# Four of sixteen feed-forward inputs transposed through DRAM and VectorE instead of TensorE, on one Trainium2 core

## The reference

```python
x = x + 0.5 * ffn(layernorm(x))      # "first"
x = x + attention(layernorm(x))      # "att"
x = x + 0.5 * ffn(layernorm(x))      # "second"

def ffn(x):                          # W_fc 512 x 128, W_proj 128 x 512
    y = square(relu(x @ W_fc.T)) @ W_proj.T
    # five steps of a leaky spiking neuron driven by y; the share of steps that spike
    return spike_count(y) / 5        # a staircase of y with five levels

def attention(x):                    # a second layer norm with gamma, beta inside
    h = layer_norm(x) * gamma + beta
    keys, values = h @ Wk.T + bk, h @ Wv.T + bv
    w = exp((keys @ Wka.T + bka) / sqrt(128))
    w = w / cumsum(w, over tokens)
    return cumsum(w * keys, over tokens) * values
```

## Time and profile before

| | |
|---|---|
| median of 3 runs | 148.91 us (148.85 to 149.03) |
| profiled execution | 148.56 us, of which the span from first to last instruction is 146.8 us |
| TensorE busy | 141.6 us, 96% of the span |
| VectorE busy | 128.8 us, 88% |
| ScalarE busy | 128.5 us, 88% |
| GpSimd busy | 95.1 us, 65% |
| granted TensorE clock | 1.000 of full speed (2.4 GHz) over the whole span |

### The profile page before, as it was taken

How to read it: one execution, slowest core, us unless ns; L and a number is a source line. 1 busy time by engine, 2 the same in 40 slices (tenths; PEclk the granted TensorE clock), 3 DMA queues, 4 the chain that set the end, 5 groups by cost and what they waited for, 6 DMA issues and landing times.

```text
span 146.8 us, 3000 instructions
## 1 busy us (share of the span) xinstructions
PE 141.6 (96%) x945; PEld 126.1 (86%) x945; DVE 128.8 (88%) x441; ACT 128.5 (88%) x255; POOL 95.1 (65%) x138
## 2 busy tenths in 40 slices
PE   7899999999999999999999999999999999999990
PEld 7599898989889889997988988889989898979780
DVE  2985478999699999999989999999989999968674
ACT  3376989999999998979999999899898988988861
POOL 1448135478899928993999899998934954580200
PEclk9999999999999999999999999999999999999999
DMA  4975000000000000000000000000000101040422
GB/s 136 273 195 165 4 2 0 0 0 7 0 0 2 2 4 0 0 0 0 4 0 2 0 0 4 2 0 0 0 4 0 55 18 58 18 143 0 143 71 72
DMA packets 10510, 5.09 MB, mean 35 GB/s; under 512 B 1152, under 2 KB 10496, under 8 KB 10496
## 3 DMA queue, kind: packets, MB, share of 16 engines
q1 hardware_dynamic: 9808, 4.53, 10.7%
q10 hardware_dynamic: 688, 0.39, 0.9%
HBM read 2.82 MB, written 2.10 MB: 34 GB/s over the span
## 4 chain that ended last, share of the span: by engine, by line
PE 92%; DMA 3%; DVE 1%; ACT 1%; ACTq 1%; issue 0%
PE work L1062 37%; PE hidden L983 11%; PE hidden L987 10%; PE hidden L984 10%; PE work L996 5%; DMA proj_raw<-in_L_ffn_W_proj_dram 3%; PE att_work L1093 3%; PE att_work L983 3%; PE att_work L984 3%; PE att_work L987 3%; PE att_value L1117 2%; PE att_value L983 1%; PE att_value L987 1%; PE att_value L984 1%; PE work L1074 1%; ACT signs L535 1%
## 5 line engine op out<-in xcount | busy, mean ns | idle before, releaser
L1062 PE MATMUL work<-proj_t,square 128*128 128x128 f32 x480 | 61.7, 276 | 0.1
L1062 PEld LDWEIGHTS work<-proj_t,square 128*128 128x128 f32 x480 | 59.0, 192 | 2.9 <-POOL square L455 0.5
L551 ACT ACTIVATE signs<-work 128x512 uint8<-128x512 f32 x63 | 35.7, 619 | 5.3 <-PE work L1062 5.3
L522 ACT ACTIVATE relu<-hidden 128x512 f32<-128x512 f32 x64 | 38.0, 627 | 0.0
L527 ACT ACTIVATE square<-relu 128x512 f32<-128x512 f32 x53 | 35.5, 670 | 0.3
L983 PE MATMUL hidden<-in_hi,fc_lo 128*128 128x512 f32 (+1 forms) x66 | 27.6, 418 | 0.1
L429 POOL TENSOR_TENSOR rstd<-var_eps,minus_half 128x4 f32<-128x4 f32 x15 | 15.3, 1021 | 16.2 <-DVE neg_mean L646 16.2
L987 PE MATMUL hidden<-in_lo,fc_hi 128*128 128x512 f32 (+1 forms) x66 | 25.6, 388 | 0.0
L984 PE MATMUL hidden<-in_hi,fc_hi 128*128 128x512 f32 (+1 forms) x66 | 25.4, 385 | 0.0
L435 POOL TENSOR_SCALAR normed<-x_second,neg_mean,rstd 128x128 f32<-128x128 f32 x32 | 16.7, 534 | 0.8
L435 POOL TENSOR_SCALAR normed_att<-x_att,neg_mean_att,rstd_att 128x128 f32<-128x128 f32 x28 | 16.2, 590 | 0.7
(11 more groups left out here) (123 smaller groups left out, 257.8 us busy)
## 6 DMA issues: line engine op xcount, KB each, us to landing
x_first<-_attn_hidden_states_dram SPq DMA_DIRECT2D x7, 256.0 KB, 4.4
out_dram<-x_out SPq DMA_DIRECT2D x7, 256.0 KB, 2.2
out_dram<-x_out SPq DMA_DIRECT2D x4, 64.0 KB, 1.5
x_first<-_attn_hidden_states_dram ACTq DMA_DIRECT2D x1, 128.0 KB, 2.7
x_first<-_attn_hidden_states_dram SPq DMA_DIRECT2D x1, 128.0 KB, 2.4
fc_raw<-in_L_ffn_W_fc_dram SPq DMA_DIRECT2D x1, 128.0 KB, 2.7
fc_raw<-in_L_ffn_W_fc_dram ACTq DMA_DIRECT2D x1, 128.0 KB, 3.3
proj_raw<-in_L_ffn_W_proj_dram SPq DMA_DIRECT2D x1, 128.0 KB, 3.5
```

What stands on the lines that cost most here:

```text
L522: nc.scalar.activation(relu[j.lane][:, c, :], bank_of_hidden(j, c)[:], ACT.Relu).then_inc(relu_made[j.lane], 1)
L551: nc.scalar.activation(planes[:, k, :], work[j.lane][:], func, bias=bias, scale=scale).then_inc(signs_made[j.lane], 1)
L1062: last = nc.tensor.matmul(work[j.lane][:, tokens], square[j.lane][:, c, tokens], proj_t[:, c, :], start=(c == 0 and t == 0), stop=(c == NC ...
```

## The change

Jobs 4 to 7 no longer go through TensorE for their transpose. `normed` is stored to a DRAM scratch and loaded back by four DMAs so that each 32 x 32 block lies in the place of its transpose, and VectorE's block transpose turns all the blocks at once (`turn_by_dma`, `turn_blocks`). `ff_hi` then reads this SBUF tile; it stands earlier in ScalarE's step, right behind `ff_relu(i, 2)`. The low part moves from VectorE to GpSimd (`ff_pool_lo`). Each of these jobs has normalisation buffers of its own, and its layer norm is computed earlier: on VectorE, job 4 in step 1, job 5 in step 2, jobs 6 and 7 in step 3; on GpSimd, job 4 in iteration 0, job 5 in iteration 1, job 6 in iteration 2 and job 7 in iteration 3. To make room, `x_of["att"]` and `x_of["out"]` become the same buffers as `x_of["first"]` and `x_of["second"]`, so that the residual adds write in place.

```diff
+DMA_TURNED = (4, 5, 6, 7)
+BLOCK = 32
...
+        self.dma_turned = i in DMA_TURNED
+        self.norm = f"dma{i}" if self.dma_turned else self.lane
+        self.norm_turn = 0 if self.dma_turned else sum(k not in DMA_TURNED for k in range(self.lane, i, 2))
...
-        KINDS = (0, 1, "att")
+        KINDS = (0, 1, "att") + tuple(FeedForward(i).norm for i in DMA_TURNED)
...
-        x_of = {k: [sb(f"x_{k}_{b}", [P, NT, P]) for b in range(NB)] for k in ("first", "att", "second", "out")}
+        x_of = {k: [sb(f"x_{k}_{b}", [P, NT, P]) for b in range(NB)] for k in ("first", "second")}
+        x_of["att"], x_of["out"] = x_of["first"], x_of["second"]
...
+            def turn_by_dma(j):
+
+                i, rows, columns = j.index, S // BLOCK, D // BLOCK
+                sp.wait_ge(normed_made[j.norm], NT)
+                sp.dma_start(scratch[i].rearrange("(t p) d -> p t d", p=P),
+                             normed[j.norm][:]).then_inc(normed_stored[i], 16)
+                sp.wait_ge(normed_stored[i], 16)
+                source = scratch[i].rearrange("(i r) (j c) -> j r i c", r=BLOCK, c=BLOCK)
+                for k in range(columns):
+                    sp.dma_start(blocks[i][k * BLOCK:(k + 1) * BLOCK, :].rearrange("r (i c) -> r i c", i=rows),
+                                 source[k]).then_inc(blocks_loaded[i], 16)
+
+            for i in DMA_TURNED:
+                turn_by_dma(FeedForward(i))
...
+            def ff_pool_lo(j):
+                pool.wait_ge(blocks_turned[j.index], 1)
+                pool.wait_ge(hi_made[j.lane], j.turn + 1)
+                pool.wait_ge(hidden_made[j.lane], NC * j.turn)
+                nc.gpsimd.tensor_tensor(in_lo[j.lane][:], turned_x[j.index][:], in_hi[j.lane][:].bitcast(F32),
+                                        ALU.subtract).then_inc(lo_made[j.lane], 1)
...
             for i in range(FIRST_STEP, STEPS):
                 for j in feed_forward(i + 2):
-                    ff_normalise(j)
+                    if not j.dma_turned and j.index != 3:
+                        ff_normalise(j)
+                if i == 0:
+                    ff_normalise(FeedForward(4))
+                if i == 1:
+                    ff_normalise(FeedForward(3))
+                if i == 2:
+                    ff_normalise(FeedForward(6))
+                if i == 3:
+                    ff_normalise(FeedForward(7))
+                for j in feed_forward(i + 2):
+                    if j.dma_turned:
+                        ff_pool_lo(j)
                 for b in attention(i + 2):
                     att_normalise(b)
+                if i == 1:
+                    ff_normalise(FeedForward(5))
...
-                act.wait_ge(turned[j.lane], j.turn + 1)
+                if j.dma_turned:
+                    act.wait_ge(blocks_turned[j.index], 1)
+                    act.wait_ge(hidden_made[j.lane], NC * j.turn)
+                    nc.scalar.activation(in_hi[j.lane][:], turned_x[j.index][:], ACT.Copy).then_inc(hi_made[j.lane], 1)
+                    return
...
                     ff_square(j, 1)
                     ff_relu(j, 2)
+                for j in feed_forward(i + 1):
+                    if j.dma_turned:
+                        ff_hi(j)
...
+            def ff_layer_norm(j):
+                ff_layer_stats(j)
+                ff_layer_args(j)
+
+            def turn_blocks(j):
+                dve.wait_ge(blocks_loaded[j.index], 16 * (D // BLOCK))
+                nc.vector.transpose(turned_x[j.index][:], blocks[j.index][:]).then_inc(blocks_turned[j.index], 1)
...
                 if i == ATT_STEP[0]:
                     first_attention_normalise()
+                    ff_layer_stats(FeedForward(6))
...
+                if i == ATT_STEP[0]:
+                    ff_layer_args(FeedForward(6))
...
                 for j in feed_forward(i):
-                    if j.index > 0:
+                    if j.index > 0 and not j.dma_turned:
                         ff_lo(j)
+                if i == 1:
+                    ff_layer_norm(FeedForward(4))
+                if i == 2:
+                    ff_layer_norm(FeedForward(5))
...
                 for b in attention(i):
                     att_part_lo(b)
+                for j in feed_forward(i + 1):
+                    if j.dma_turned:
+                        turn_blocks(j)
...
                 for b in attention(i):
                     att_sum(b)
+                if i == 3:
+                    ff_layer_norm(FeedForward(7))
...
             def ff_turn(j):
 
+                if j.dma_turned:
+                    return
...
             def ff_contract(j, c):
+                if j.dma_turned and c == 0:
+                    pe.wait_ge(signs_made[j.lane], j.before(lambda other: other.sign_parts))
```

More of the change, by code:

```diff
@@ L206, in macaron_kernel @@
     FIRST_STEP = -3
-    EPS_OF = {0: LN_EPS, 1: LN_EPS, "att": LN_EPS * LN_EPS / (1.0 + LN_EPS)}
+    ATT_EPS = LN_EPS * LN_EPS / (1.0 + LN_EPS)
     ATT_GAMMA_SCALE = 1.0 / math.sqrt(1.0 + LN_EPS)
@@ L266, in macaron_kernel @@
         normed = {k: sb(f"normed_{k}", [P, NT, P]) for k in KINDS}
+        assert S % BLOCK == 0 and D % BLOCK == 0
+        blocks = {i: sb(f"blocks{i}", [P, S]) for i in DMA_TURNED}
+        turned_x = {i: sb(f"turned_x{i}", [P, S]) for i in DMA_TURNED}
+        scratch = {i: nc.dram_tensor(f"scratch{i}", (S, D), F32) for i in DMA_TURNED}
         in_hi = [sb(f"in_hi{l}", [P, S], F32R) for l in LANES]
@@ L333, in macaron_kernel @@
         pooled_made, attended_made, attended_turned = sem("pooled_made"), sem("attended_made"), sem("attended_turned")
+        normed_stored = {i: sem(f"normed_stored{i}") for i in DMA_TURNED}
+        blocks_loaded = {i: sem(f"blocks_loaded{i}") for i in DMA_TURNED}
+        blocks_turned = {i: sem(f"blocks_turned{i}") for i in DMA_TURNED}
         def flat(tile):
@@ L441, in ff_normalise @@
                 else:
-                    normalise(j.lane, j.turn, x_of[j.layer][j.batch])
+                    normalise(j.norm, j.norm_turn, x_of[j.layer][j.batch])
+            def ff_pool_lo(j):
[4 more added lines that the diff above has]
+                                        ALU.subtract).then_inc(lo_made[j.lane], 1)
             def att_normalise(b):
@@ L516, in ff_hi @@
                     return
-                act.wait_ge(turned[j.lane], j.turn + 1)
+                if j.dma_turned:
[3 more added lines that the diff above has]
+                    return
+                act.wait_ge(turned[j.lane], j.norm_turn + 1)
                 nc.scalar.activation(in_hi[j.lane][:], work[j.lane][:], ACT.Copy).then_inc(hi_made[j.lane], 1)
@@ L621, in _ @@
                 for j in feed_forward(i + 1):
-                    ff_hi(j)
+                    if not j.dma_turned:
+                        ff_hi(j)
                     if j.index == 0:
@@ L672, in ff_layer_stats @@
                     dve.wait_ge(x_made["second"], j.batch + 1)
-                layer_stats(j.lane, j.turn, x_of[j.layer][j.batch])
+                layer_stats(j.norm, j.norm_turn, x_of[j.layer][j.batch])
             def ff_layer_args(j):
-                layer_args(j.lane, j.turn)
+                layer_args(j.norm, j.norm_turn)
+            def ff_layer_norm(j):
[4 more added lines that the diff above has]
+                nc.vector.transpose(turned_x[j.index][:], blocks[j.index][:]).then_inc(blocks_turned[j.index], 1)
             def att_layer_stats(b):
@@ L897, in _ @@
             for kind in KINDS:
-                nc.vector.memset(moments[kind][:, :, 2:3], EPS_OF[kind]).then_inc(consts_made, 1)
+                nc.vector.memset(moments[kind][:, :, 2:3], ATT_EPS if kind == "att" else LN_EPS).then_inc(consts_made, 1)
             nc.vector.memset(ones[:, P:S], 1.0).then_inc(consts_made, 1)
@@ L917, in _ @@
                         other_fc_low_parts()
-                    else:
+                    elif not j.dma_turned:
                         ff_layer_stats(j)
@@ L993, in ff_turn @@
                 for t in range(NT):
-                    pe.wait_ge(normed_made[j.lane], NT * j.turn + t + 1)
+                    pe.wait_ge(normed_made[j.norm], NT * j.norm_turn + t + 1)
                     bank_of = first_second_half if j.index == 0 and t >= HALF_TILES else work[j.lane]
-                    last = nc.tensor.transpose(bank_of[:, t * P:(t + 1) * P], normed[j.lane][:, t, :], ident[:])
+                    last = nc.tensor.transpose(bank_of[:, t * P:(t + 1) * P], normed[j.norm][:, t, :], ident[:])
                     if j.index == 0 and t == HALF_TILES - 1:
@@ L999, in ff_turn @@
                         turn_proj(range(0, NC // 2))
-                last.then_inc(turned[j.lane], 1)
+                last.then_inc(turned[j.norm], 1)
             def turn_proj(chunks):
```

## The result

The changed kernel takes **155.67 us** (median of 6 runs, 155.40 to 157.04), the kernel before 148.95 us beside it (6 runs, 148.71 to 149.33). The ratio is 1.0464, with a 95% interval of 1.0431 to 1.0497: 4.6% slower. The forecast was 155.8 us.

A forecast was written before the change was run, and what follows sets the result against it. TensorE sets the pace, with ScalarE as full; the low part closes a loop of ScalarE and GpSimd. Delays reach 6.9 us: 148.56 + 6.9 = 155.5 us, by the median 155.8 us, range 150.5 to 158.4 us.

The forecast's parts named there:

- The closed loop: ScalarE and GpSimd wait for each other from step 4 on; one turn 11.6 us against 9.37 before; chance 0.73.
- the path of the sum: Delays of `att_turn` grow over steps 4, 5 and 7 to 6.9 us, which stays to the end.
- The lead of 0.6 us in step 2: VectorE does job 5's layer norm before `att_layer_stats(0)`, so `first_attention_normalise`, then TensorE and ScalarE, run 0.6 us late.
- the guess of step 6: On ScalarE, batch 2's guess comes 0.5 us later because `ff_hi(6)` now stands ahead of it.
- the listed sign: TensorE idle 2 us or more in front of L1093 in each of steps 4, 5 and 7, released by GpSimd.
- three signs of being wrong: TensorE idle under 1.8 us in steps 4 to 7; `in_hi` of job 4 well before 34 us; `turn_blocks` awaiting loads.
- The other signs: GpSimd idle ahead of the low part, `att_off_square` released by the guess sum, no VectorE DMA wait behind step 2.
- The block transposes at nothing: On VectorE, 0.7 us each, adding nothing because VectorE has 1.36 us to spare in step 4.
- The DMA path: Store lands in 2.2 us, the four loads in 3.5 to 8.8 us; taken as hidden.
- The late-loads rival: VectorE stops at `turn_blocks(5)` if the four loads take over 8.4 us; 159.4 us at 12 us; chance 0.05.
- The pure gain: `att_normalise` stays off the path and TensorE keeps its 1.76 us: 147.15 us; chance 0.11.
- Half of the loop: One or two of the three waits are covered as ScalarE runs ahead; step 4 alone gives 150.2 us; chance 0.09.

The follow-up runs named there:

- E1: The changed kernel with GpSimd's low part behind `att_normalise` instead of ahead of it, nothing else changed: 151.97 us.
- E9: The changed kernel with only job 6's low part on GpSimd, those of jobs 4, 5 and 7 back on VectorE: 151.92 us.
- E10: The changed kernel with only job 5's low part on GpSimd, those of jobs 4, 6 and 7 back on VectorE: 153.18 us.
- E2: The changed kernel with the low part of jobs 4 to 7 back on VectorE at its old place, reading SBUF: 152.03 us.
- E5: As E2, with `in_hi` of jobs 4 to 7 back near the end of ScalarE's step, behind the last square: 150.33 us.
- E4: The kernel before with only the earlier layer norms, their own buffers and in-place sums; transposes on TensorE, no DMA path: 149.68 us.
- E8: The kernel before plus four VectorE block transposes that nobody reads, one in each of steps 3 to 6: 151.74 us.
- E7: As E6, with `in_hi` of jobs 4 to 7 written by VectorE right behind the block transpose: 152.02 us.
- E6: As E5, with moved layer norms in slots of the kernel before, one step sooner, and block transposes behind `att_share_key`: 150.74 us.
- E3: The changed kernel with GpSimd doing each of the four low parts twice, the first into a tile nobody reads: 161.37 us.

## Why the prediction was right, step by step

*What sets the time.* The prediction said of the low part that "on GpSimd it stands in front of `att_normalise`, whose result those three `att_turn` wait for". This is shown by E1, where the order alone is worth 3.7 us, and by E9 against E10. But it is not the whole of the slowdown, as the prediction had it. The rest, about 3 us, came to light only in E1, E2 and E5.

*The closed loop.* One turn, from `att_off_square(0)` to `(1)`, took 54.31 - 42.98 = 11.33 us (predicted 11.6, before 9.37). `att_turn` was late by 2.62, 4.46 and 6.78 us (predicted 2.59, 4.52 and 6.89). `att_off_square(2)` came at 64.06 - 1.69 = 62.37 us (62.65), and in sum nothing was won or lost after step 7. So the path of the sum is the one that the trace shows. The durations held too: block transpose 0.70 us (0.7), low part 1.28 (1.27), `in_hi` 0.65 (0.63). `att_normalise` was 2.93, 2.90 and 3.04 us, near the lower bound, and not 3.29. That the sum is right to 0.1 us is in part luck: these three are 1.0 us shorter together than was added up, and most of that was paid back by a longer lead (0.77 us in place of 0.6) and by the way from the start of `in_hi` to the low part, 0.8 us in each turn in place of 0.63.

*The lead of 0.6 us in step 2.* Size about right, place wrong. `first_attention_normalise` starts at 29.19 - 1.69 = 27.50 instead of 27.33 us, only 0.17 later. The rest came in step 3: the low part of job 3 on VectorE stands behind the layer norm of job 6, and TensorE waits 0.43 us for it (L1069). ScalarE passed `ff_relu(3, 2)` at 36.76 - 1.69 = 35.07 instead of 34.30 us, 0.77 late. E4 prices the moved layer norms at 0.6 us in all.

*What the prediction didn't see.* It counted `in_hi` as a link of GpSimd's loop and, but for the guess of step 6, not as a cost for ScalarE's other customers. The signs, the square and the guess that now stand behind it come later, and TensorE waits for the square: 0.76 us in step 4, 0.46 in step 5, 0.24 and 0.46 in step 6, though no row of before shows such a wait. With the low part out of the way (E2) that is what gates, and moving `in_hi` back is worth 1.7 us (E5). By the timeline the loop's length covered it in the changed kernel: TensorE waited for the square first and for `normed` right behind it, and the second wait ended when GpSimd was done, whatever the first one took. For the same reason the listed sign, 2 us or more in front of L1093, failed as it was worded: TensorE's loss in step 4 is 0.76 us at the square, 0.44 ahead of `att_turn` and 1.53 - 0.60 = 0.93 inside it, 2.1 us in all, and 1.8 us in step 5 by the same three rows. In step 7 there are 1.5 us at `att_turn` alone. None of the three signs of being wrong came: TensorE's idle time ahead of its groups in steps 4 to 7 is 3.4 us by the rows above, over the 1.8 asked for. The other signs came true: idle time ahead of the low part, `att_off_square` released by the guess sum, and no wait of VectorE for a DMA behind step 2.

*The block transposes at nothing.* The number fits the changed kernel, where VectorE gives up four `in_lo` of 0.67 us for four transposes of 0.70 us, and waits in any case (3.10 us ahead of `att_lo` in step 4). The reason given, 1.36 us to spare in step 4, is not enough: it doesn't hold for steps 5 to 7, where VectorE has 0.03 us in 20. E8 shows that without the exchange they have a price, 2.8 us by the medians and 1.8 us by its trace. So the change had the choice between two prices, each more than the 1.76 us that TensorE saves: leave the low part on VectorE (E5 to E7 lose 1.2 to 2.9 us against before), or hand it to GpSimd in front of `att_normalise`. None of the versions run beats the kernel before. What E5 still loses, 1.2 us although TensorE has 1.76 us less to do, isn't split: the layer norms (E4), VectorE's added work (E8) and the stretched low parts (E6) are on record as costs, and how much is due to each stays open.

*The DMA path.* Hidden, as forecast. In the trace the loads for job 5 are issued from 34.22 us on over 1.90 us and land about 2.3 us after issue; its transpose starts at 43.37 us. The late-loads rival is out. The Trainium skill's rule that a plain strided copy is 19 times slower than the transposing path ("VectorE: DVE Perf Modes", "The three transpose paths") is stated for a large innermost stride at the destination, which the prediction left out. It doesn't bite in this form, in which 128 bytes stay together: 64 KB landed in 2.3 us, against 2.2 us for the plain 256 KB store.

*The other rivals.* The pure gain needed under 2.42 us from `in_hi` to the end of `att_normalise(1)`; it took 4.9. Half of the loop needed a covered wait; all three stand in the trace.

## What to carry to other kernels

When an instruction goes onto an in-order engine, price what stands behind it there as well: the same low part cost nothing where no one wanted the next instruction (E9) and 1.26 us where TensorE did (E10). Before calling an engine idle enough, look at it in each stage that gets new work; VectorE's 88% over the span was 100% in the 20 us that mattered. And when the longest wait is removed, expect the next one to stand right behind it: here ScalarE's `in_hi` was hidden by GpSimd's loop until that was gone.

## What the runs showed of the hardware

- A longer wait can cost more than its length, through the clock. In E3 the granted clock fell to 0.59 in the 4 us behind a stretch in which TensorE was busy for 2.07 us, and to 0.86 in a stretch with 2.93 busy us and 0.72 in the next. The second fall, with no wait behind it, cost 1.3 us. It doesn't follow every wait: after 2.37 busy us in another 4 us the clock of E3 stayed at 1.00. No run here shows what decides it.
- Of two elementwise instructions with two SBUF operands each, one on VectorE and one on GpSimd, the one that starts second is stretched: in E6 a low part that started 0.70 us before `guess_sum` ended took 1.26 in place of 0.67 us, and `guess_share`, started while it ran, 1.74 in place of 1.29. In E2, where the low parts of jobs 4 to 6 started first, they took 0.66 to 0.68 us and `guess_sum` 1.51 to 1.68. This agrees with the Trainium skill ("SBUF — State Buffer", "SBUF: two separate sides"), which has one hold the port pair for its whole instruction while the other waits. A low part that reads PSUM didn't have this cost: 0.66 to 0.69 us in the kernel before, with `guess_share` beside it at 1.29 to 1.30.
- A block transpose of 128 x 512 fp32 on VectorE took 0.70 us in the changed kernel and in E8, about as long as a subtraction of that size.
